# Two cross-attentions of a perceiver: value products moved ahead of the next value projection, and ScalarE's first key copies moved ahead of a square root

## The reference

```
x = x + L0_xattn(layernorm(x), ctx)      # 16 heads of 16, relative positions
x = x + L0_attn(layernorm(x))            # causal attention on a latent
x = x + L0_ffn(layernorm(x))             # 8 experts, top 2, and a shared one
x = x + L1_xattn(layernorm(x), ctx, mask)
x = x + L1_attn(...)                     # gated delta rule, and an MLP
x = x + L1_ffn(x)                        # blockwise FP4 linear layers
```

```
q = x @ Wq + bq;  k = ctx @ Wk + bk;  v = ctx @ Wv + bv        # per head: 16 wide
p = softmax(q k^T / 4)                                        # over 1601 keys
x = x + (p v) @ Wo + bo
```

## Time and profile before

| what | value |
|---|---|
| time, median of 3 runs | 2751.24 us (2748.86 to 2752.64) |
| the profiled execution's own time | 2750.76 us |
| its span, first to last instruction | 2748.9 us |
| TensorE busy | 2479.6 us (90%) |
| VectorE busy | 1401.1 us (51%) |
| ScalarE busy | 1025.5 us (37%) |
| GpSimd busy | 570.8 us (21%) |
| mean granted TensorE clock | 0.96 of full speed |

### The profile page before, as it was taken

How to read it: one execution, slowest core, us unless ns; L and a number is a source line. 1 busy time by engine, 2 the same in 40 slices (tenths; PEclk the granted TensorE clock), 3 DMA queues, 4 the chain that set the end, 5 groups by cost and what they waited for, 6 DMA issues and landing times. The chain is left out here.

```text
span 2748.9 us, 91354 instructions
## 1 busy us (share of the span) xinstructions
PE 2479.6 (90%) x41697; PEld 1780.7 (65%) x41697; DVE 1401.1 (51%) x2289; ACT 1025.5 (37%) x1382; POOL 570.8 (21%) x440
## 2 busy tenths in 40 slices
PE   7999999999998877868999999999789998998798
PEld 4666766766666555536666666666567777777466
DVE  4454454454453862255545454545555555554378
ACT  2333333333333431124444444444434454444223
POOL 2424423423431203121010101010011111111000
PEclk9999999999999669989999999999989999999899
DMA  2111111111111321121111111111100000000200
GB/s 93 32 38 32 32 38 32 32 38 32 32 32 65 120 84 62 48 79 32 44 32 43 33 38 32 44 32 58 54 2 3 4 3 4 3 4 4 81 1 16
DMA packets 56729, 102.31 MB, mean 37 GB/s; under 512 B 10272, under 2 KB 49024, under 8 KB 55024
## 3 DMA queue, kind: packets, MB, share of 16 engines
q1 hardware_dynamic: 54448, 91.35, 10.8%
q0 software_dynamic: 1904, 5.15, 0.5%
HBM read 90.30 MB, written 9.21 MB: 36 GB/s over the span
## 5 line engine op out<-in xcount | busy, mean ns | idle before, releaser
L653 DVE TENSOR_REDUCE x_mx<-banks 128x2 f32<-128x800 f32 (+1 forms) x512 | 505.5, 990 | 160.8 <-PE banks L798 133.1
L823 PE MATMUL banks<-x_wv,x_cT 128*128 128x256 f32 (+1 forms) x1664 | 418.9, 393 | 12.3 <-DVE x_nmb L660 12.3
L728 PE MATMUL banks<-x_cT,x_wk 128*128 128x400 f32 (+1 forms) x1024 | 386.3, 520 | 17.4 <-ACT x_kT L476 11.4
L823 PEld LDWEIGHTS banks<-x_wv,x_cT 128*128 128x128 f32 (+1 forms) x1664 | 296.3, 187 | 83.6 <-issue 24.5
L539 ACT ACTIVATE x_PT<-banks 128x2048 f32<-128x2048 f32 (+1 forms) x112 | 196.6, 1755 | 369.2 <-PE banks L858 369.2
L541 ACT ACTIVATE x_PT<-banks,x_kbs 128x1024 f32<-128x1024 f32 (+1 forms) x208 | 221.3, 1111 | 289.0 <-PE banks L858 289.0
L671 DVE COPY x_V<-banks 128x512 f32<-128x512 f32 (+1 forms) x224 | 146.2, 653 | 336.6 <-PE banks L823 336.3
L728 PEld LDWEIGHTS banks<-x_cT,x_wk 128*128 128x128 f32 x1024 | 189.8, 194 | 149.2 <-issue 35.8
L858 PE MATMUL banks<-x_qbd,x_kT 32*128 32x128 f32 x6656 | 248.0, 272 | 0.0
L858 PEld LDWEIGHTS banks<-x_qbd,x_kT 32*128 32x128 f32 x6656 | 243.6, 182 | 3.5
L840 PE MATMUL banks<-x_PT,x_V 128*32 128x64 f32 x13312 | 234.0, 221 | 6.0 <-issue 5.2
(11 more groups left out here) (402 smaller groups left out, 3586.1 us busy)
## 6 DMA issues: line engine op xcount, KB each, us to landing
x_cT<-in_ctx SPq DMA_DIRECT2D x96, 400.0 KB, 3.6
x_cT<-in_ctx SPq DMA_DIRECT2D x32, 401.0 KB, 3.6
e_up<-in_mo_up SPq DMA_DIRECT2D x9, 512.0 KB, 15.4
e_down<-in_mo_down SPq DMA_DIRECT2D x9, 512.0 KB, 16.2
x_mrow<-in_mask_row SPq DMA_DIRECT2D x1, 3202.0 KB, 14.4
t_w<-in_db_w SPq DMA_DIRECT2D x3, 1024.0 KB, 7.1
e_rows<-in_c_unfilled SPq DMA_DIRECT2D x1, 2967.0 KB, 13.1
e_xg<-e_rows SPq DMA_DIRECT2D x23, 129.0 KB, 2.0
```

Of the source, the lines that this page charges most:

```text
L653: dve.reduce_max(mx[:, H0[k]:H0[k] + 3:2, kb], g.PS[:, first:first + 2, 0:KBS[kb]], AXX).then_inc(max_read, 1)
L728: last = pe.matmul(PJ[pb][:, 0:KBS[k]], wk[:, c, gg, :], cT[:, (p + 1) % 2, c, KB0[k]:KB0[k] + KBS[k]], start=c == 0, stop=c == KC - 1)
L823: last = pe.matmul(PJ[pb][0:CHK[c + k], D * k:D * k + D], cT[:, p, cc, 128 * (c + k):128 * (c + k) + CHK[c + k]], wv[:, cc, :], start=cc = ...
```

## The change

It has two parts. In each pair the products A stand ahead of the projection P, so that a pair reads S M1 A M2 P M3; the numbers of the maxima stay 1, 2, 3, and the two tables trade their values. VectorE's list gets the three reductions first and `values(c + 2)` last. In the masked attention ScalarE copies three key blocks before the root and the fourth after it (in the first attention `rooted` is 0, and the order stays).

```diff
         SCORED = {2: 1, 4: 4, 6: 7, 8: 10, 10: 13}
-        PROJECTED = {0: 0, 2: 2, 4: 5, 6: 8, 8: 11, 10: 14}
-        VALUED = {2: 3, 4: 6, 6: 9, 8: 12, 10: 15}
+        VALUED = {2: 2, 4: 5, 6: 8, 8: 11, 10: 14}
+        PROJECTED = {0: 0, 2: 3, 4: 6, 6: 9, 8: 12, 10: 15}
...
-            ln_root(act, g, n)
-            act.wait_ge(wk_in, 32)
+            rooted = NKB - 1 if mask else 0
             for k in range(NKB):
+                if k == rooted:
+                    ln_root(act, g, n)
+                if k == 0:
+                    act.wait_ge(wk_in, 32)
                 key_block(Bank(SECT[0][2]), SECT[0][1][0], 1, k, 0)
...
                     if ahead and c in SCORED:
                         maximum(SCORED[c])
+                    if ahead and c in VALUED:
+                        maximum(VALUED[c])
+                    if ahead and c in PROJECTED:
+                        maximum(PROJECTED[c])
                     if c + 2 < NCH:
                         values(c + 2)
-                    if ahead and c in PROJECTED:
-                        maximum(PROJECTED[c])
-                    if ahead and c in VALUED:
-                        maximum(VALUED[c])
...
                         scores(c)
                         if ahead and c in SCORED:
                             maximum(SCORED[c])
+                        for a in (c - 2, c - 1) if c else ():
+                            attend_values(a)
+                        if ahead and c in VALUED:
+                            maximum(VALUED[c])
                         if c + 2 < NCH:
                             project_values(c + 2)
                         if ahead and c in PROJECTED:
                             maximum(PROJECTED[c])
-                        for a in (c - 2, c - 1) if c else ():
-                            attend_values(a)
-                        if ahead and c in VALUED:
-                            maximum(VALUED[c])
```

## The result

The changed kernel takes 2710.34 us (median of four runs, 2706.03 to 2715.56) beside 2751.94 us for the kernel before (four runs, 2748.86 to 2753.12): a ratio of 0.9845, 95% interval 0.9829 to 0.986. That is 42 us faster. The forecast was 2728 us and its range 2714 to 2742: the direction is right, the time lies 3.7 us under the low end. The profiled execution is the slowest of the four, 2715.56 us with a span of 2713.7.

The account below looks back on a forecast made before the run. TensorE, busy 90%, was taken as the bound, losing 44.9 us in 120 maxima waiting for VectorE's reductions behind a copy. Loop 19.5 plus head 4.0 made 23.5 us, hence 2728 us, range 2714 to 2742.

Parts of the forecast that it names:

- The loop: Batch loops of both attentions: reordered pairs gain 19.5 us, 11.3 in the masked and 8.2 in the first attention.
- pair 2, M1 to M3: Second pair of a batch: no copy before M1's reduction in the masked attention, 0.30 us gained; 0.09 in the first.
- M3 of pair 2 to M3 of pair 8: Three pairs of a masked batch: 16.33 us falls to 15.72, 0.61 gained, a middle pair taking 5.24 us.
- pair 10, M3 to M3: Pair projecting only 65 keys: 4.31 us becomes 4.47, 0.16 lost, pair 8's copy now being before its M1.
- The head: Masked attention's start: 8.2 us gained, less 2.1 for held adds and 2.1 for the clock, 4.0 us; between -0.5 and 8.2.
- Keys no longer limiting: Masked head: key blocks end earlier, so the query projection starts at 1198.5 instead of 1206.73, 8.2 us gained.
- The hold of the adds: Masked head: GpSimd's products hold VectorE's adds L572, once in full and once in part, 2.1 us lost; bounds 0 and 5.1.
- The clock: Masked head: TensorE, after standing idle, runs at half speed for a while, 2.1 us lost; bounds 0 and 3.6.
- A: Rival: in the loop M2 waits where M3 waited, nothing gained there, only the head remains; 2747 us, chance 0.07.
- B: Rival: VectorE's loop chain from M3 to next M2 is longer, 3.47 us, slower from 3.23 on; about 2781 us, chance 0.05.
- C: Rival: the loop's queued copy takes under 0.61 us and TensorE's 2.92 us bounds; 13 us more gained, 2715 us, chance 0.13.
- D: Rival: loop as forecast, head gives nothing, products holding the moments too and projection at half clock; 2732 us, chance 0.15.

Follow-up runs that it names:

- VectorE's part alone: Kernel before, TensorE's order untouched, VectorE's copy of the values moved between the reductions of M2 and M3: 2723.27 us, ratio 0.9906.
- the doubled copy: Changed kernel with every copy of values but a batch's first made twice on VectorE, one to a scratch tile: 2788.08 us, ratio 1.0129.
- the copy on ScalarE: Changed kernel with the copies of values moved from VectorE to ScalarE, behind the exponentials: 2700.35 us, ratio 0.981.
- the repetition: The changed kernel measured once more, nothing altered, beside the kernel before: 2704.59 us, ratio 0.9838.
- the head part alone: Kernel before with only ScalarE's reordering of key copies and root in the masked head, loop as before: 2746.05 us, ratio 0.9976.

## Why the prediction came out as it did

**What bounds the kernel: right.** The copy ahead of a reduction across A was the stall. The kernel with VectorE's part alone takes it away without moving P; the chain M3, copy, reduction of M1, M2 sets the new pair, as the doubled copy and the copy on ScalarE show from both sides.

**The loop: right mechanism, sized at half.** This is the step that failed: 19.5 us forecast, 39.1 measured, 32.9 of them in the steps. Term by term, in us a batch:

```
                                 forecast           measured
                             masked   first     masked   first
pair 2, M1 to M3               0.30    0.09       0.33    0.09
M3 of pair 2 to M3 of pair 8   0.61    0.62       0.83    0.83
pair 10, M3 to M3             -0.16   -0.16      -0.07   -0.07
maximum 0 to M1 of pair 2      0       0          0.16    0.09
sum                            0.75    0.55       1.25    0.94
batch period                                      1.24    0.95
```

Three sizes were off. The link from a reduction to the copy behind it was taken as 1.00 us from the one row that had it, and it is 0.91; with M2 to M3 at 2.20 in place of 2.21 that makes the 0.2 us of the middle pairs and pair 10's 0.09. That row was the last copy of a batch, 256 elements wide, and the neighbouring numbers scatter in steps of 0.09; one row should have given a bound, not the value. (Pair 6 gained nothing by it: its M3 to M2 is 3.02 us, 0.09 more than in pairs 8 and 10, and why stays open.) The pair before pair 2 was not worked out at all: S "alone" was read as 1.28 us from 1388.98 to 1390.26, but that maximum was itself late, because maximum 0's reduction had a copy before it. Without it the same distance is 1.12 us (1410.54 to 1411.66 in the kernel after). The idle time did not show, since S's matmuls were drawn over it.

That error also misled the balance of the two engines. TensorE's length of M3 to M2 was put at 2.80 to 2.92 us from 0.27 + 1.28 + 1.37; measured it is 2.86, so the range held.

**What no term had: 7.0 us of stops inside the products**, the waits for TensorE's instructions shown above. The page of the kernel before showed them as idle time of L840 put down to "issue", and the forecast bounded the loop by the 44.9 us of waits for VectorE only. The change takes them away by the order of pair 10, the very pair for which a loss was forecast; the kernel before with that order alone is 6.3 to 7.4 us faster. With the steps, 32.9 + 7.0 = 39.9 against 39.1 between the landmarks. Of the 19.6 us that the forecast of the loop lacked, these stops are the largest part, 7.0; the middle pairs lacked 6.4, pair 0 3.8 and pair 10 2.7.

**The head: 4.0 forecast, 4.1 measured, by sizes that cancel.** That the sum fits is luck; four of its sizes were off. Keys no longer limiting was put at 8.2 us and gave 7.2: from the last normed tile to the query projection it was 9.55 us and is 2.31, where 1.3 had been taken. The transposes between them, before (x16) and after (x12), show why:

```profile
1203.83 1.97 PE L176 MATMUL banks<-ident,XN 128*128 128x128 f32 x16
```

```profile
1180.68 2.77 PE L176 MATMUL banks<-ident,XN 128*128 128x128 f32 x12 [1.38 <-DVE XN L98]
```

The granted clock was 1.00 in the first and 0.53 in the second. The hold of the adds was put at 2.1 and took 2.8. The clock was put at 2.1. It is most of the 1.0 us just named, in the repetition and in the head part alone as well (twelve transposes in 2.82 us at 0.50), and a slow query projection cost 1.7 more in this profile and nothing in those two. And 1.3 us of gain was missed: with the copies ahead of it the root's table load is over before the moments are, so the root starts 0.2 us behind L93. Together: 8.2 - 1.0 - 2.8 - 1.7 + 1.3 = 4.0.

**The rivals.** A (the loop gains little) and B (slower) fell: no pair reached 3.23 us; their chance of 0.12 together was fair, and the doubled copy shows that B's mechanism is real, at 0.60 us more a chain. C (more is gained, 2715 us) was nearest in time, and right that the two bounds lie close (0.07 us apart where it can be seen), but for another reason than it gave: the copy takes 0.60 us until the next reduction, as priced, and the link before it was the shorter one. D (the head gives nothing) fell.

**The range.** It was built from mishaps of the loop downward (7.5 us as the lower bound) and from one small surprise upward. Nothing in it covered unread idle time of TensorE.

## What to carry to other kernels

Where two engines hand banks to each other, ask of each instruction of the slower link what stands ahead of it in its queue while its data are ready: exchanging two instructions on VectorE gave 26 of the 42 us here, without touching TensorE. Before bounding a gain by the wait that the change aims at, list all idle time inside the groups that move, "issue" too, and work out every distance between landmarks, not only those with a wait in their row. And when an engine's work is brought forward, look at what it now runs beside: here one semaphore wait that keeps GpSimd's products out of VectorE's adds was worth 4.5 us.

## What the runs showed of the hardware

- TensorE stopped inside dense runs of small matmuls (64 in 1.10 us) without waiting for a semaphore, and seven of thirty batches were 0.46 to 1.43 us longer for it. It waited for its own instructions: it went on 1.25 to 1.48 us behind the landing of a 16 KB packet, at number 193 or 194 of a group of 256, each time. With a projection of four matmuls, 1.08 us, between the last two of these runs no stop was left.
- On VectorE an instruction behind a PSUM reduction of 128x800 (0.99 us) started 0.91 us after the reduction's start when its data were ready, and the one behind a copy of 128x512 shown as 0.68 us after 0.60. Chains of ready instructions are shorter than the sum of the durations shown.
- The same kernel ran the sixteen matmuls of the query projection in 7.11 or in 8.79 us, by the clock granted in its first microseconds (0.55 or 1.00 of full speed).
- ScalarE's table load of 1.28 us is off the path when copies stand in front of the root and it is done before the root's input is written: the root then starts 0.2 us behind its input.
